# State-space projection stage: the long GpSimd passes move to VectorE and ScalarE, and one of TensorE's two convolved channel tiles moves to VectorE

## The reference

```python
xz = hidden_states @ W_in
x, z = jnp.split(xz, 2, axis=-1)
x = jax.lax.conv_general_dilated(x, conv_w[:, None, :], (1,), [(D_CONV - 1, 0)], ...)   # 4 taps, one channel each
x = silu(x + conv_b)
proj = x @ W_x
dt_low = proj[..., :DT_RANK]
Bm, Cm = proj[..., DT_RANK:DT_RANK + D_STATE], proj[..., DT_RANK + D_STATE:]
dt = jax.nn.softplus(dt_low @ W_dt + b_dt)
```

## Time and profile before

| what | value |
|---|---|
| median of 3 runs | 3557.52 us (3557.5 to 3559.53) |
| profiled execution, its own time | 3564.47 us |
| span of the profiled execution, first to last instruction | 3562.7 us |
| busy in the span: TensorE matmul | 3187.8 us (89%) |
| VectorE | 2460.8 us (69%) |
| ScalarE | 1846.6 us (52%) |
| GpSimd | 1413.2 us (40%) |
| mean granted TensorE clock | 0.954 |

### The profile page before, as it was taken

How to read it: one execution, slowest core, us unless ns; L and a number is a source line. 1 busy time by engine, 2 the same in 40 slices (tenths; PEclk the granted TensorE clock), 3 DMA queues, 4 the chain that set the end, 5 groups by cost and what they waited for, 6 DMA issues and landing times. The chain is left out here.

```text
span 3562.7 us, 52184 instructions
## 1 busy us (share of the span) xinstructions
PE 3187.8 (89%) x18048; PEld 1963.4 (55%) x18048; DVE 2460.8 (69%) x4614; ACT 1846.6 (52%) x3943; POOL 1413.2 (40%) x967
## 2 busy tenths in 40 slices
PE   8699999979999899999999899898288888888878
PEld 5344444346666555566666555443156565555777
DVE  8588887657777632277777433389699999999543
ACT  2177776836666511166666311265467777777111
POOL 4201111132222211032222211133599999999443
PEclk9799999989999999999999999999699999999979
DMA  6946576110020043000110123144444242420776
GB/s 184 158 59 96 79 98 119 32 35 23 23 66 24 26 160 99 26 20 23 38 52 21 46 65 86 51 138 146 175 160 185 78 176 83 174 92 36 259 264 222
DMA packets 262786, 347.27 MB, mean 97 GB/s; under 512 B 70427, under 2 KB 181513, under 8 KB 261884
## 3 DMA queue, kind: packets, MB, share of 16 engines
q1 hardware_dynamic: 248924, 308.30, 30.9%
q10 hardware_dynamic: 9120, 23.35, 1.9%
q0 software_dynamic: 4480, 12.30, 0.9%
HBM read 227.72 MB, written 112.80 MB: 96 GB/s over the span
## 5 line engine op out<-in xcount | busy, mean ns | idle before, releaser
L2417 POOL TENSOR_TENSOR H_feed<-H_ndu,H_bs 128x1024 f32<-128x1024 f32 x256 | 595.1, 2368 | 6.2 <-DMA H_bs<-between_bc 4.1
L896 ACT ACTIVATE B_probs<-B_p_exp,B_key_bias 128x512 f32<-128x512 f32 (+3 forms) x768 | 394.3, 582 | 159.7 <-PE B_p_exp L956 129.2
L791 DVE TENSOR_REDUCE B_part_max<-B_p_max 128x1 f32<-128x512 f32 (+3 forms) x768 | 374.6, 545 | 73.5 <-PE B_p_max L920 70.9
L1304 ACT ACTIVATE D_probs<-D_scores,D_neg,D_rq 128x256 f32<-128x256 f32 x512 | 282.9, 573 | 255.4 <-DVE D_neg L1225 255.4
L2388 ACT ACTIVATE H_decay<-H_ndt,H_rate 128x1024 f32<-128x1024 f32 x256 | 287.8, 1126 | 195.5 <-DVE H_turning L2470 103.0
L1668 PE MATMUL E_p_ag<-E_hT,FA_w 128*128 128x512 f32 x640 | 283.9, 603 | 1.9 <-ACT E_hT L1624 1.9
L917 PE MATMUL B_p_max<-BF_k,BF_q 100*128 100x512 bf16 (+3 forms) x768 | 256.9, 341 | 22.9 <-DVE B_future_b L780 12.4
L2470 DVE TENSOR_TENSOR_SCAN H_turning<-H_decay,H_feed 128x1024 f32<-128x1024 f32 x112 | 253.5, 2274 | 21.4 <-POOL H_feed L2417 18.7
L953 PE MATMUL B_p_exp<-BF_q,BF_k 100*128 100x512 bf16 (+3 forms) x768 | 250.5, 330 | 19.8 <-DMA BF_q<-B_shift_rows 13.0
L2521 PEld LDWEIGHTS H_p_y<-H_minus,H_sT 128*128 128x128 f32 x1792 | 225.5, 200 | 75.8 <-ACT H_sT L2373 55.7
L2521 PE MATMUL H_p_y<-H_minus,H_sT 128*128 128x128 f32 x1792 | 233.7, 287 | 35.4 <-ACT H_sT L2373 35.4
(11 more groups left out here) (277 smaller groups left out, 6835.8 us busy)
## 6 DMA issues: line engine op xcount, KB each, us to landing
H_bs<-between_bc SPq DMA_DIRECT2D x64, 512.0 KB, 8.1
H_cs<-between_bc SPq DMA_DIRECT2D x36, 512.0 KB, 8.9
BF_q<-between_q_parts SPq DMA_DIRECT2D x90, 128.0 KB
BF_k<-between_k_parts SPq DMA_DIRECT2D x90, 128.0 KB
between_slots_x<-E_clear ACTq DMA_DIRECT2D x4, 2570.0 KB, 18.9
I_xe<-between_slots_x ACTq DMA_DIRECT2D x32, 257.0 KB, 6.2
LA_base<-between_z SPq DMA_DIRECT2D x64, 128.0 KB, 2.2
between_z<-D_z SPq DMA_DIRECT2D x64, 128.0 KB, 1.7
```

Source lines behind the costliest of these rows:

```text
L791: nc.vector.reduce_max(part_max[:, g % 2, kc, qb, h:h + 1], p_max[:, use % 3, 0:keys], AX.X).then_inc(maxed, 1)
L896: nc.scalar.activation(probs[:, x % PROBS, skip:512], p_exp[:, n % SCORES, skip:512], ACT.Exp, bias=key_bias[:, g % SETS, kb - 4 * Q + 4, ...
L1304: last = nc.scalar.activation(probs[:, place[m], :, :].rearrange("p a b -> p (a b)"), scores[:, place[m], :, :].rearrange("p a b -> p (a b ...
L2417: nc.gpsimd.tensor_tensor(feed[:, n % AHEAD, :], ndu[:, g % 2, :], bs[:, s, :], ALU.mult).then_inc(fed, 1)
```

## The change

Four things are changed, all in `phase_front`.

1. `ON_PE` becomes one channel tile and `ON_DVE` three: TensorE issues 8 matmul instructions fewer per chunk (of 16), VectorE one more multiply and three more multiply-adds per chunk. ScalarE's Silu count is the same.
2. GpSimd keeps the small work (setting up, and the inverse deviation of 128x4) and loses all passes over 2048 columns.
3. The series is written another way: ScalarE squares (0.5·ex - 1/3), which is ex²/4 - ex/3 + 1/9, and VectorE adds 7/18 and multiplies by ex, then takes 1 minus that, times ex. VectorE's pass L1990 goes; it gets the mask (`pick`) and, for all chunks, `ndu`.
4. ScalarE's drain between |lin| and exp becomes a semaphore, and its tail is ordered anew: |lin| of chunk 6 stands ahead of the copy of the last low-rank rows.

```diff
-        ON_PE = (0, 1)
-        ON_DVE = (2, 3)
+        ON_PE = (0,)
+        ON_DVE = (1, 2, 3)
...
@@ GpSimd
-            def series(k):
-                lg, ex, poly = of_logs(k)
-                pool.wait_ge(ex_ready, k + 1)
...
-                nc.gpsimd.tensor_scalar(poly[:, :, :], ex[:, :, :], -0.25, 1.0 / 3, ALU.mult, ALU.add).then_inc(series_ready, 1)
-                reached(pool, ndt_ready, k - 1)
-                nc.gpsimd.tensor_scalar(pick[:, k % 2, :, :], ex[:, :, :], SMALL, None, ALU.is_lt).then_inc(pick_ready, 1)
-
-            def inputs(k):
-                pool.wait_ge(ndt_ready, k + 1)
...
-            for k in range(K + 2):
-                if k + 1 < K:
-                    inverse(k + 1)
-                if 2 <= k <= K:
-                    series(k - 2)
...
+            for k in range(1, K):
+                inverse(k)
@@ VectorE
-            def logs_first(k):
+            def series(k):
                 lg, ex, poly = of_logs(k)
-                dve.wait_ge(series_ready, k + 1)
-                nc.vector.tensor_tensor(poly[:, :, :], poly[:, :, :], ex[:, :, :], ALU.mult)
+                dve.wait_ge(ex_ready, k + 1)
+                nc.vector.tensor_scalar(pick[:, k % 2, :, :], ex[:, :, :], SMALL, None, ALU.is_lt)
+                dve.wait_ge(square_ready, k + 1)
+                nc.vector.scalar_tensor_tensor(poly[:, :, :], poly[:, :, :], 7.0 / 18, ex[:, :, :], ALU.add, ALU.mult)
                 dve.drain()
-                nc.vector.scalar_tensor_tensor(poly[:, :, :], poly[:, :, :], -0.5, ex[:, :, :], ALU.add, ALU.mult)
...
+                nc.vector.scalar_tensor_tensor(poly[:, :, :], poly[:, :, :], 1.0, ex[:, :, :], ALU.subtract, ALU.mult,
+                                               reverse0=True)
...
-            def inputs_last(k):
+            def inputs(k):
                 dve.wait_ge(ndt_ready, k + 1)
-                dve.wait_ge(ndu_stored[k % 2], 16 * (k // 2))
+                reached(dve, ndu_stored[k % 2], 16 * (k // 2))
                 nc.vector.tensor_tensor(ndu[:, k % 2, :, :], ndt[:, k % 2, :, :], xs[:, k % 3, :, :], ALU.mult
                                         ).then_inc(ndu_ready, 1)
...
                 if k >= 2:
-                    logs_first(k - 2)
-                    logs_second(k - 2)
-            dve.wait_ge(ndu_ready, K - 1)
-            inputs_last(K - 1)
+                    series(k - 2)
+                    step(k - 2)
+                    inputs(k - 2)
@@ ScalarE
-                nc.scalar.activation(lg[:, :, :], lin[:, k % 2, :, :], ACT.Abs)
-                act.drain()
+                nc.scalar.activation(lg[:, :, :], lin[:, k % 2, :, :], ACT.Abs).then_inc(size_ready, 1)
...
+            def squares(k):
+                lg, ex, poly = of_logs(k)
+                act.wait_ge(ex_ready, k + 1)
+                if k == K - 2:
+                    act.wait_ge(xn_ready, K)
+                nc.scalar.activation(poly[:, :, :], ex[:, :, :], ACT.Square, bias=third[:, 0:1], scale=0.5
+                                     ).then_inc(square_ready, 1)
...
                 if k >= 1:
                     put_lin(k - 1, 1)
+                if k >= 2:
+                    squares(k - 2)
                 put_xs(k)
...
+            magnitudes(K - 2)
+            put_low(K - 1)
             exps(K - 2)
-            put_low(K - 1)
+            squares(K - 2)
             logs(K - 2)
             put_lin(K - 1, 0)
             put_lin(K - 1, 1)
+            magnitudes(K - 1)
             exps(K - 1)
+            squares(K - 1)
             logs(K - 1)
```

More of the change, by code:

```diff
@@ L1769, in phase_front @@
         power = a.sb("power", [P, CT])
+        third = a.sb("third", [P, 1])
         stats = a.sb("stats", [P, CT, 6])
@@ L1809, in phase_front @@
         lin_ready = a.sem("lin_ready")
+        size_ready = a.sem("size_ready")
         ex_ready = a.sem("ex_ready")
         lg_ready = a.sem("lg_ready")
-        series_ready = a.sem("series_ready")
-        pick_ready = a.sem("pick_ready")
+        square_ready = a.sem("square_ready")
         ndt_ready = a.sem("ndt_ready")
@@ L1893, in _ @@
             nc.gpsimd.memset(power[:, :], -0.5)
+            nc.gpsimd.memset(third[:, :], -1.0 / 3)
             nc.gpsimd.memset(w_low[:, :, :], 0.0)
@@ L1902, in inverse @@
                 nc.gpsimd.tensor_tensor(rstd[:, k % 2, :], spread[:, :], power[:, :], ALU.pow).then_inc(rstd_ready, 1)
-            def series(k):
-                lg, ex, poly = of_logs(k)
-                pool.wait_ge(ex_ready, k + 1)
[L1907 to L1910, removed]
-                nc.gpsimd.tensor_scalar(poly[:, :, :], ex[:, :, :], -0.25, 1.0 / 3, ALU.mult, ALU.add).then_inc(series_ready, 1)
-                reached(pool, ndt_ready, k - 1)
-                nc.gpsimd.tensor_scalar(pick[:, k % 2, :, :], ex[:, :, :], SMALL, None, ALU.is_lt).then_inc(pick_ready, 1)
-            def inputs(k):
-                pool.wait_ge(ndt_ready, k + 1)
-                reached(pool, ndu_stored[k % 2], 16 * (k // 2))
-                nc.gpsimd.tensor_tensor(ndu[:, k % 2, :, :], ndt[:, k % 2, :, :], xs[:, k % 3, :, :], ALU.mult
-                                        ).then_inc(ndu_ready, 1)
             inverse(0)
@@ L1985, in convolve, with step @@
                 last.then_inc(conv_ready, 1)
-            def logs_first(k):
+            def series(k):
                 lg, ex, poly = of_logs(k)
-                dve.wait_ge(series_ready, k + 1)
-                nc.vector.tensor_tensor(poly[:, :, :], poly[:, :, :], ex[:, :, :], ALU.mult)
+                dve.wait_ge(ex_ready, k + 1)
+                nc.vector.tensor_scalar(pick[:, k % 2, :, :], ex[:, :, :], SMALL, None, ALU.is_lt)
+                dve.wait_ge(square_ready, k + 1)
+                nc.vector.scalar_tensor_tensor(poly[:, :, :], poly[:, :, :], 7.0 / 18, ex[:, :, :], ALU.add, ALU.mult)
                 dve.drain()
-                nc.vector.scalar_tensor_tensor(poly[:, :, :], poly[:, :, :], -0.5, ex[:, :, :], ALU.add, ALU.mult)
-            def logs_second(k):
+                nc.vector.scalar_tensor_tensor(poly[:, :, :], poly[:, :, :], 1.0, ex[:, :, :], ALU.subtract, ALU.mult,
+                                               reverse0=True)
+            def step(k):
                 lg, ex, poly = of_logs(k)
                 dve.drain()
-                nc.vector.scalar_tensor_tensor(poly[:, :, :], poly[:, :, :], 1.0, ex[:, :, :], ALU.add, ALU.mult)
-                dve.drain()
                 dve.wait_ge(lg_ready, k + 1)
-                dve.wait_ge(pick_ready, k + 1)
                 nc.vector.copy_predicated(lg[:, :, :], pick[:, k % 2, :, :], poly[:, :, :])
@@ L2003, in logs_second @@
                 reached(dve, ndt_stored[k % 2], 16 * (k // 2))
-                reached(dve, ndu_ready, k - 1)
                 nc.vector.scalar_tensor_tensor(ndt[:, k % 2, :, :], lin[:, k % 2, :, :], 0.0, lg[:, :, :],
                                                ALU.min, ALU.subtract).then_inc(ndt_ready, 1)
-            def inputs_last(k):
+            def inputs(k):
                 dve.wait_ge(ndt_ready, k + 1)
-                dve.wait_ge(ndu_stored[k % 2], 16 * (k // 2))
+                reached(dve, ndu_stored[k % 2], 16 * (k // 2))
                 nc.vector.tensor_tensor(ndu[:, k % 2, :, :], ndt[:, k % 2, :, :], xs[:, k % 3, :, :], ALU.mult
@@ L2085, in put_xs_last, with magnitudes @@
                                          ).then_inc(xs_ready, 1)
-            def exps(k):
+            def magnitudes(k):
                 lg, ex, poly = of_logs(k)
@@ L2094, in exps @@
                     reached(act, ndt_ready, k if k < K - 1 else k - 1)
-                nc.scalar.activation(lg[:, :, :], lin[:, k % 2, :, :], ACT.Abs)
-                act.drain()
+                nc.scalar.activation(lg[:, :, :], lin[:, k % 2, :, :], ACT.Abs).then_inc(size_ready, 1)
+            def exps(k):
+                lg, ex, poly = of_logs(k)
+                act.wait_ge(size_ready, k + 1)
                 nc.scalar.activation(ex[:, :, :], lg[:, :, :], ACT.Exp, scale=-1.0).then_inc(ex_ready, 1)
+            def squares(k):
+                lg, ex, poly = of_logs(k)
+                act.wait_ge(ex_ready, k + 1)
[3 more added lines that the diff above has]
+                                     ).then_inc(square_ready, 1)
             def logs(k):
@@ L2106, in _ @@
                 if k >= 2:
+                    magnitudes(k - 2)
                     exps(k - 2)
```

## The result

The changed kernel takes 3524.1 us (median of 5 runs, 3520.8 to 3529.35) where the one before takes 3557.52: a ratio of 0.9904, 95% interval 0.9893 to 0.9915. Measured once more beside other kernels it is 0.9894 (0.9875 to 0.9912). The forecast was 3521 us, a ratio of 0.9897. The profiled execution took 3528.04 us with a span of 3526.2.

What follows compares the result with a forecast made beforehand. No engine bounds the whole stage: TensorE bounds early turns, VectorE those from turn 3, with 8.9 us each GpSimd's. -6.7 - 14.2 - 15.7 = -36.6 us takes 3557.5 to 3520.9, say 3521 us; range 3516 to 3530.

Steps and rivals of the forecast that it cites:

- VectorE was held by GpSimd: Steady turns: GpSimd's passes hold VectorE's normalisation 6.8 us and delay the inverse deviation 2.06 us, 8.9 us per turn.
- Rival 3: Steady turns: the long normalisation is not GpSimd's doing, the 6.8 us stay, about 3561 us; chance 0.03.
- First term: Up to the first `ndt`, in turn 2: projections start 7.0 us earlier, `ndt` of chunk 0 ends at 2350.0, -6.7 us.
- Second term: Five steady turns, `ndt` of chunk 0 to chunk 5: 28.0 us each, 140.0 against 154.24, -14.2 us.
- rival 1: Steady turns: TensorE's clock falls once in each, 1.8 us on eight projections, 9 us on top, 3530 us; chance 0.08.
- ScalarE's chain: Steady turn: |lin| to last `lin`, square, then VectorE's two passes, copy and `ndt`, 28.0 us, longer than VectorE alone, 27.1.
- Third term: Stage's end, `ndt` of chunk 5 to the last `ndu`: 29.3 us against 45.0, -15.7 us.
- The mask: Mask on VectorE over 2048 columns into int32: priced at 1.2 us by the nearest one-input multiply, with 2.29 possible.
- rival 2: The mask is as slow on VectorE as on GpSimd, 6.5 us, giving 3554 us, no difference; chance 0.03.
- Rival 4: Steady turns: TensorE stays at its lower clock, turns take 46.4 us, 3613 us, slower; chance 0.04.
- my signs of being wrong: Mask over 2.3 us, table load ahead of the square, granted clock below 1 in steady turns, or turns set by TensorE's projections.
- The sum: Whole kernel: the three stage savings add to -36.6 us, profile-to-median difference of 6.95 us carried unchanged, 3521 us.

Runs made afterwards that it cites:

- the early square: The changed kernel with ScalarE's square moved from behind the last `lin` to directly behind exp, ahead of the logarithm: ratio 0.9860 to the kernel before, stage 249.0 us.
- the first experiments: Three runs: kernel before with only the tile moved, 1.0020; changed kernel with the tile not moved, 0.9921; changed kernel with the mask on GpSimd, 0.9939.
- the probe: The changed kernel with unread GpSimd int32 passes beside VectorE's nine multiply-adds, memset in turns 3 and 4, read-and-write in 5 and 6: nine took 6.38 and 9.81 us.

## Why the prediction was right

*VectorE was held by GpSimd.* Shown from both sides: the normalisation fell from 8.19 to 1.38 us with the passes gone, rose to 6.54 with one given back, and stayed at 8.19 with the tile alone moved. Rival 3 falls.

*First term, -6.7 us:* turn 2's projections started at 2317.37, forecast 2317.15, and `ndt` of chunk 0 ended at 2350.05, forecast 2350.0; measured from the stage's own start -6.9. The wait for the square was 5.06 us.

*Second term, -14.2:* -13.9. Four turns took 27.7 us where I had 28.0. The fifth took 29.4, by the slow stretch of rival 1, which came once and not five times. The two errors cancel, and that is luck: the forecast had no such stretch, rival 1 had five, and no run explains the one. That ScalarE's chain, not VectorE's, set the turn was shown by the early square, which took the waits away and left VectorE's own chain. My 27.1 for that chain was 26.6.

*Third term, -15.7:* -16.8. A mask and the first series pass are 1.14 us apart and the masked copy is shorter at the end. I had 13.5 us per chunk, it was 12.95.

*The mask:* 1.22 us against my 1.2, and rival 2 falls. That is about half of the 2.29 us of a two-input pass over the same columns, so no cost of the int32 output shows; the same pass with a float output was not run. Pricing it by the row of the taps was right. The two-port rule of the Trainium skill ("VectorE: DVE Perf Modes", section "Mode 2×_2P — use both read ports for one tensor") has one-input instructions at double rate too, and 1.22 against 2.29 agrees.

*Rival 4* did not come: the granted clock of the steady turn was 1.00. A clock below 1 in a steady turn was among my signs of being wrong; in the fifth turn it showed, 0.68 over one group of projections.

*The sum* was -36.6; the stage gave -37.7, the profiled executions -36.4, and the medians -33.4. The difference lies outside the stage: 1.2 us in the rest of the profiled execution, 3.0 in the step to the median. There I carried the 6.95 us between profile and median of the kernel before over unchanged, and for the changed kernel it was 3.9. That offset comes from one profiled execution of each kernel, and single executions spread by more: beside the first experiments those of the kernel before lie between 3554.9 and 3573.8 us. In the second measurement the medians lie 40.1 us apart. That the forecast came within 3 us of the first is therefore in part luck; what is shown is the stage.

## What to carry to other kernels

A long busy time for a short instruction can be a hold: compare the same instruction in a turn where the other engine is idle before counting it as work. Two halves of a change can need each other: moving a tile to VectorE cost 7 us of the stage while GpSimd held VectorE and gained 16 once it did not. When an engine's work goes elsewhere, look where in that engine's order the new instruction stands: the square cost 9.4 us only by standing behind `lin`.

## What the runs showed of the hardware

GpSimd's mask of 2048 columns into int32 took 5.38 us, its pass from float to float 1.90; VectorE's mask took 1.22.

Beside GpSimd's int32 pass, VectorE's one-input instructions lost 5.2 us of 5.4, and a two-input one 3.4 of 5.4. Beside a memset of 1.8 us, which only writes, the two-input ones lost nothing. How long a two-input instruction is held depended on GpSimd's pass: beside the int32 passes it went on 1.9 us before the end of GpSimd's row (twice in the probe, twice at the end of the kernel before), beside the float product `ndu` 0.15 us before it (6.57 us instead of 2.29, mask on VectorE in the kernel before). Ends of GpSimd's rows are rough, and why the two differ is not shown.

The Trainium skill ("SBUF — State Buffer", section "Who interferes with whom") says that an instruction with two SBUF inputs contends with a GpSimd instruction that reads SBUF, not with one that only writes it: the runs agree. It also says that an instruction in a two-port mode and GpSimd hold the shared ports against each other for the whole instruction: the one-input normalisation agrees, with 5.2 of 5.4 us lost.

VectorE's copies out of PSUM ran at 0.68 us each and its statistics at 0.74 for two beside GpSimd's two-input product of 4.5 us, as alone.
